# A mixture-of-experts layer stores its results by slot and gathers them by token

## What is computed

```python
logits = jnp.einsum('btc,ec->bte', x, router_w)
top_vals, top_idx = jax.lax.top_k(logits, TOP_K)          # TOP_K = 2
gates = jax.nn.sigmoid(top_vals)
w_full = jnp.zeros((N, E)).at[jnp.arange(N)[:, None], sel].add(gw)
gate, up = jnp.split(jnp.einsum('nc,ech->neh', xf, gate_up_w), 2, axis=-1)
out_all = jnp.einsum('neh,ehc->nec', silu(gate) * up, down_w)
moe = jnp.einsum('ne,nec->nc', w_full, out_all)
x = x + moe + shared                                      # then layer 1's attention reads layernorm(x)
```

## Time and profile before

| | |
|---|---|
| median of 3 runs | 944.12 us (941.67 to 946.22) |
| the profiled execution, its own time | 942.74 us |
| its span, first to last instruction | 940.3 us |
| mean granted TensorE clock | 0.964 |
| PE busy | 807.3 us (86%) |
| DVE busy | 607.4 us (65%) |
| ACT busy | 380.0 us (40%) |
| POOL busy | 238.6 us (25%) |
| POOL, gathers of line 1827 | 87 in both layers, 92.3 us |
| POOL, scatters of line 1834 | 48, 50.3 us |

### The profile page before, as it was taken

The page is one execution under the profiler, slowest core; times in us unless marked ns, Lnnn a source line. Parts: engine busy times, 40 slices in busy tenths (PEclk is TensorE's granted clock), DMA queues, the critical chain, the costliest instruction groups (busy, mean ns, idle before and its releaser), DMA issues.

```text
span 940.3 us, 23518 instructions
## 1 busy us (share of the span) xinstructions
PE 807.3 (86%) x8622; PEld 600.3 (64%) x8623; DVE 607.4 (65%) x1398; ACT 380.0 (40%) x750; POOL 238.6 (25%) x203
## 2 busy tenths in 40 slices
PE   5998998999977777779899999983659999999992
PEld 3655555655666666665545666663339899999992
DVE  3446777588645555555965888868965655555651
ACT  3325555533222212124314666666334444444440
POOL 0012000100146565651030000011034444444531
PEclk9999999999999999999997999996779999999997
DMA  8967302244442222228535411149232333333344
GB/s 265 104 82 114 125 3 71 88 148 154 135 136 84 73 80 77 78 73 222 88 45 73 90 47 48 47 161 381 91 123 56 71 72 70 68 68 68 72 66 112
DMA packets 72975, 94.68 MB, mean 101 GB/s; under 512 B 14321, under 2 KB 58225, under 8 KB 72881
## 3 DMA queue, kind: packets, MB, share of 16 engines
q1 hardware_dynamic: 57088, 62.17, 27.6%
q0 software_dynamic: 13872, 29.24, 12.4%
q10 hardware_dynamic: 1952, 2.39, 0.8%
HBM read 63.09 MB, written 19.92 MB: 88 GB/s over the span
## 4 chain that ended last, share of the span: by engine, by line
PE 60%; DVE 18%; issue 7%; another core or an unknown queue 5%; ACT 3%; DMA 2%; SPq 1%; DVEq 1%; POOLq 0%; ACTq 0%
PE bank L920 13%; PE bank L933 11%; PE bank L701 4%; PE bank L722 3%; PE bank L839 3%; PE bank L826 3%; PE bank L829 3%; PE bank L670 3%; PE bank L519 3%; PE bank L533 3%; PE bank L562 2%; DVE arena L1673 2%; DVE neg_max L1376 2%; DVE arena L1708 2%
## 5 line engine op out<-in xcount | busy, mean ns | idle before, releaser
L920 PE MATMUL bank<-arena 128*128 128x128 f16 x3024 | 303.8, 220 | 2.8 <-DVE arena L1678 2.0
L933 PE MATMUL bank<-arena 128*128 x1224 | 281.2, 273 | 5.1 <-DVE arena L1686 1.9
L920 PEld LDWEIGHTS bank<-arena 128*128 x3024 | 263.5, 98 | 20.4 <-issue 4.4
L1827 POOL DMA_INDIRECT arena<-xn_d,get_i x87 | 92.3, 1061 | 179.4 <-DVE arena L1673 79.1
L1241 ACT ACTIVATE arena<-bank,arena 128x128 f32<-128x128 f32 x312 | 85.9, 378 | 124.8 <-DMA arena<-in_exp_b 77.2
L1376 DVE TENSOR_REDUCE neg_max<-bank 128x2 f32<-128x512 f32 (+1 forms) x180 | 117.4, 684 | 28.0 <-PE bank L670 27.9
L933 PEld LDWEIGHTS bank<-arena 128*128 128x128 f16 x1224 | 119.4, 98 | 18.2 <-issue 16.6
L1111 ACT ACTIVATE arena<-bank 128x1024 f32<-128x1024 f32 x96 | 96.7, 1026 | 16.7 <-PE bank L688 16.1
L1837 POOL DMA_INDIRECT sum_d<-arena,put_i x39 | 64.0, 1642 | 111.2 <-DVE arena L1699 105.2
L1686 DVE TENSOR_TENSOR arena<-arena 128x512 f16<-128x512 f32 (+1 forms) x126 | 74.6, 592 | 4.3
L519 PE MATMUL bank<-consts 128*128 128x256 f32 (+2 forms) x144 | 53.5, 502 | 26.5 <-DVE slot L1577 18.0
(11 more groups left out here) (187 smaller groups left out, 1144.8 us busy)
## 6 DMA issues: line engine op xcount, KB each, us to landing
arena<-arena SPq DMA_DIRECT2D x96, 128.0 KB, 5.2
arena<-in_exp_up SPq DMA_DIRECT2D x16, 512.0 KB, 3.7
arena<-in_exp_dn SPq DMA_DIRECT2D x6, 1024.0 KB, 6.8
arena<-in_exp_up SPq DMA_DIRECT2D x5, 1024.0 KB, 5.9
arena<-in_exp_b SPq DMA_DIRECT2D x39, 128.0 KB
arena<-in_ctxT SPq DMA_DIRECT2D x8, 512.0 KB, 10.4
arena<-in_exp_dn SPq DMA_DIRECT2D x16, 256.0 KB, 4.0
xn_d<-arena POOLq DMA_DIRECT2D x8, 512.0 KB, 5.6
```

The source lines that it names most:

```text
L920: last = mm(upP[u][:, m // (UB // 2), m % (UB // 2) * P:(m % (UB // 2) + 1) * P], weights(e, 0, w, k * UPW[l] + m * P, P), rowsT[u][x][:, ...
L933: last = mm(yP[u], hidT[u][x][:, k], weights(e, 1, w, k * D, D), start=n == 0, stop=n == n_second - 1)
L1827: pool.indirect_dma_start(rows[i % 2], None, xn_d[l], bass.IndirectOffsetOnAxis(ap=get_i[:, i:i + 1], axis=0)).then_inc(s["rows_in"][i % 2 ...
```

## The change

Layer 0's results are no longer scattered. SP stores each tile as it is, 128 slots in a row of DRAM, with one plain DMA per tile, as soon as DVE has written it. POOL keeps only the gets in layer 0's loop; the puts of layer 1 are as before. At the start of layer 1 POOL, not SP, brings the results back: for each chunk, rank and token tile one indirect DMA that gathers 128 rows of `y_d` by `slot`, 32 in all. DVE's combine waits for all 8 of its chunk. The index arithmetic for empty slots falls away: they all fetch one of the first 128 tokens' rows, and nobody reads their results.

```diff
-        ranked_d = dram("ranked_d", (RANKED + 2 * N, D), F32)
+        y_d = dram("y_d", (NS[0] * P, D), F32)
...
-                if l:
-                    load_results(0, 2)
                 sp.wait_ge(once["far_set"], l + 1)
...
                     keys(1, 0)
-                    load_results(2, NC)
                     keys(1, 1)
...
-            def load_results(lo, hi):
+            def store_results():
                 s = B[0]
-                for u in range(RESULTS[0]):
-                    sp.wait_ge(s["y_stored"][u], (NS[0] + RESULTS[0] - 1 - u) // RESULTS[0] * 16)
-                for c in range(lo, hi):
-                    after(sp, s["gathered"][c % 2], c // 2 * 2 * 16)
-                    for i in range(2):
-                        sp.dma_start(y_got[c][:, i], by_token(ranked_d[RANKED + i * N:RANKED + (i + 1) * N], c)).then_inc(s["gathered"][c % 2], 16)
+                for i in range(NS[0]):
+                    sp.wait_ge(s["y_ready"], i + 1)
+                    sp.dma_start(y_d[i * P:(i + 1) * P], y_rows[i % 4]).then_inc(s["y_stored"][i % 4], 16)
...
                     load_context(1, 0, NC)
+                    store_results()
...
+                v.tensor_scalar(pad[0][:, 0:S], tile_of, 0.0, pcol[:], ALU.is_equal, ALU.mult)
                 if l:
-                    v.tensor_scalar(pad[0][:, 0:S], tile_of, 0.0, pcol[:], ALU.is_equal, ALU.mult)
                     v.tensor_scalar(pad[1][:, 0:S], tile_of, 0.0, float(N), ALU.is_equal, ALU.mult)
-                else:
-                    chain.then(v.tensor_scalar(pad[1][:, 0:S], tile_of, 0.0, None, ALU.is_equal))
-                    v.tensor_tensor(pad[0][:, 0:S], pad[1][:, 0:S], slot_no[:, 0:S], ALU.mult)
...
-                dve.wait_ge(s["gathered"][g % 2], (g // 2 + 1) * 2 * 16)
+                dve.wait_ge(s["gathered"][g % 2], (g // 2 + 1) * 2 * TC * 16)
...
+            def gather_results():
+
+                s = B[0]
+                for u in range(RESULTS[0]):
+                    pool.wait_ge(s["y_stored"][u], (NS[0] + RESULTS[0] - 1 - u) // RESULTS[0] * 16)
+                for c in range(NC):
+                    after(pool, s["gathered"][c % 2], c // 2 * 2 * TC * 16)
+                    for i in range(2):
+                        for t in range(TC):
+                            pool.indirect_dma_start(y_got[c][:, i, t], None, y_d, bass.IndirectOffsetOnAxis(
+                                ap=slot[:, i, c * TC + t:c * TC + t + 1], axis=0)).then_inc(s["gathered"][c % 2], 16)
...
+                if l:
+                    gather_results()
                 pool.wait_ge(once["bias_step"], l * 5 + 4)
...
-                for i in range(S + BEHIND):
+                for i in range(S + BEHIND if l else S):
                     if i < S:
                         get(i)
-                    if i >= BEHIND:
+                    if l and i >= BEHIND:
                         put(i - BEHIND)
```

More of the change, by code:

```diff
@@ L83, in dram @@
             return nc.dram_tensor(name, shape, dt, kind="Internal").ap()
-        RANKED = 48 * P
+        TOKENS = 48 * P
         xn_d = [dram(f"xn_d{l}", (N, D), F32) for l in range(2)]
-        ranked_d = dram("ranked_d", (RANKED + 2 * N, D), F32)
+        y_d = dram("y_d", (NS[0] * P, D), F32)
         sum_d = dram("sum_d", (N + P, D), F32)
@@ L198, in xattn_moe_program @@
         tile_col = sb("tile_col", [P, 2, 2 * T], I32)
-        slot_no = sb("slot_no", [P, 48])
         pad = [sb(f"pad{l}", [P, 48]) for l in range(2)]
@@ L1763, in _ @@
             v.tensor_copy(inv_val[:, :, 0], pcol[:].to_broadcast([P, 2 * T])).then_inc(once["iota_ready"], 1)
-            v.tensor_copy(inv_val[:, :, 1], iota_b[:, RANKED // P:RANKED // P + 2 * T]).then_inc(once["iota_ready"], 1)
-            v.tensor_scalar(slot_no[:], iota_b[:, 0:48], float(P), pcol[:], ALU.mult, ALU.add).then_inc(once["iota_ready"], 1)
-            dve.wait_ge(once["iota_ready"], 5)
+            v.tensor_copy(inv_val[:, :, 1], iota_b[:, TOKENS // P:TOKENS // P + 2 * T]).then_inc(once["iota_ready"], 1)
+            dve.wait_ge(once["iota_ready"], 4)
             for l in range(2):
@@ L1831, in put @@
                     pool.wait_ge(s["y_ready"], i + 1)
[L1832 to L1837, removed]
+                    after(pool, s["y_stored"][1 - i % 2], (i + 1) // 2 * 16)
+                    pool.indirect_dma_start(sum_d, bass.IndirectOffsetOnAxis(ap=put_i[:, i:i + 1], axis=0),
+                                            y_rows[i % 2], None, compute_op=ALU.add).then_inc(s["y_stored"][i % 2], 16)
                 BEHIND = 5
-                for i in range(S + BEHIND):
+                for i in range(S + BEHIND if l else S):
                     if i < S:
                         get(i)
-                    if i >= BEHIND:
+                    if l and i >= BEHIND:
                         put(i - BEHIND)
```

## The result

The changed kernel takes 934.34 us (median of 13 runs, 929.88 to 943.82) against 943.24 for the kernel before (13 runs, 937.84 to 951.97): ratio 0.9913, 95% interval 0.9884 to 0.9941. It is 0.9% faster and lies inside the range of 901 to 944, but 31 us were forecast and 9 came. The profiled execution took 932.53 us.

The account below looks back on a forecast made before the run. Layer 0's loop was taken to be bound by gathers queued behind POOL's scatters and late PE signals. Loop -38.6, gathers +6.9, clock +1: -30.7 from 942.74 gives 912.0, stated as 913 us; range 901 to 944.

Parts of the forecast that it names:

- Both causes named: Layer 0's expert loop: gathers queued behind scatters on POOL and late PE signals lengthen a step to 3.37 us.
- the first rival: Loop: PE's signals stay late, only the wait for rows goes; 925 to 943 us; chance 0.17.
- The third rival: Projection: DVE's operations hold up POOL's gathers; 917 us if mild, whole 38.6 gain eaten if severe, severe chance 0.04.
- chunk 0 is complete at 427.6 + 7 x 1.27 + 2.8: Projection: chunk 0's eight gathers, 1.27 us apart, the last landing 2.8 after issue, complete at 439.3.
- T + 45: Projection: fourth combine forecast to start about 45 us after T, the end of layer 0's last evacuation.
- the gathers' term: Projection: 32 gathers on POOL replacing SP's 8 loads cost 6.9 us; bounds 0 to 11.8.
- Chunk 3 ... 6.9 us late, and everything behind it in the projection hangs on that chunk: Projection: chunk 3's gathers complete at 469.8 against 462.95, delaying everything behind by 6.9 us.
- The 1 us for the clock: Projection: 1 us added for a lower granted clock after PE's new pauses; bounds 0 and 3.
- The second rival: Loop as long as before while gathers cost; 951 to 959 us, or down to 945; chance 0.12.

Follow-up runs that it names:

- session 3: Kernel before, unchanged, 943.61 us with late signals; beside it before again 943.82, changed 937.72, plain puts on POOL 938.02, gathers in bursts of 8 929.47.
- session 6: Kernel before 912.34 us with signals in time; beside it the changed kernel 917.65 and the changed kernel with gathers in bursts of 16 921.56.
- session 4: Kernel before 941.38 us with late signals; beside it changed 933.05, its gathers in bursts of 16 920.84, memset pauses between chunks 928.01.
- session 1: Kernel before 945.58 us, late signals; changed kernel with no gather 911.71, indirect stores on POOL 971.8, one gather in flight 979.26, stack copies held back 940.66.
- session 2: Kernel before 913.78 us, signals in time; changed kernel with bursts of 8 930.44, of 4 932.81, plain loads from POOL 910.51, plain puts 919.37.

## Why the prediction was right and wrong

**Right: the loop.** A step was forecast at 2.45 and is 2.51. Steps 4 to 44 save 34.5 us (forecast 36.8), step 44 1.06 (1.1). Step 4 begins 0.8 us later than in the trace of before, where 0.7 earlier was forecast; step 2 waits 0.94 us for its rows. (In the trace of the kernel before from session 3, step 4 begins at 279.15, as late as here, so this is not the change's doing.) Together, with the last steps, 35.1 of 38.6. Both causes named, rows queued behind scatters and late signals, went away with the scatters; the first rival, signals that stay late in the loop, is refuted. Where signals are in time the step goes only from 2.65 to about 2.5. So the late signals were the larger part of what the loop had to gain, and the queue the smaller.

**Right: the stores and the pace.** SP's store lands in 1.7 us, the first gather is issued 392.21 - 389.73 = 2.5 us after T (forecast 2.8), and the 32 gathers are (431.78 - 392.21) / 31 = 1.28 us apart (forecast 1.27). Each lasts 0.95 to 1.20 us. The third rival, gathers that crawl, is not seen here. By the rule of the Trainium skill, "SBUF — State Buffer", section "SBUF: two separate sides", GpSimd can't write descriptors while VectorE runs a two-port perf-mode operation. In this trace DVE's work beside the gathers costs at most 0.25 us a gather; which of its operations are of that kind no row says.

**A size: the landing.** The step "chunk 0 is complete at 427.6 + 7 x 1.27 + 2.8" took the landing of a single get. Eight on end are noticed 406.79 - 401.03 = 5.8 us after the last one's issue. Without late signals the fourth combine is at T + 47.8, not T + 45 (the prediction's 38.6 for before counts from the start of the last evacuation, its 45 from the end): the term is 9.5 us and not 6.9.

**Wrong: the gathers' term as a whole.** The step that failed is "Chunk 3 ... 6.9 us late, and everything behind it in the projection hangs on that chunk". It priced 32 indirect DMAs, 0.3 us apart, by POOL's own time. The prediction had named late signals as something that starts when indirect DMAs follow each other on POOL with 0.3 us between them, and then moved the same pattern, 32 in a row, to a place where PE, ACT and DVE pass each other work all the time. There it costs 26.2 - 9.5 = 16.7 us more, and the fourth combine hangs not on its chunk, which had landed, but on signals. The bounds of the term (0 to 11.8) did not hold the 26.2 measured. The 1 us for the clock is in part within these 26.2: the granted clock was 0.57 from 420 to 440, where PE idles, against 1.00 in the same stretch of session 6. The forecast missed the gain by 22 us: 3.5 in the loop, the rest here.

**Luck: the range.** Its upper end was moved from 925 to 944 to take in the first rival, signals that stay late in the loop. The 934 lies where that rival put it (925 to 943), but the loop's signals were in time; others, in the projection, were late.

**Wrong: the sign is not the kernel's alone.** The forecast took the late signals for a property of the kernel before. They depend on the condition of a session as well. The second rival, slower because of the gathers, holds where signals are in time, by its own rule: a step gains less than 0.2 us (2.65 to 2.51), which is less than the gathers cost. Why some sessions have late signals is open; the chip number is excluded, nothing else was tried. What delays a semaphore's change is open too: the runs show when it is late and what brings it on, not the mechanism. Nor does a count of DMAs on end explain all of it: in the loop POOL had only four on end (store, get, store, get) and then 1.76 us of idleness, and one signal in each such round was 1.7 to 2.0 us late, where eight gathers on end did nothing.

## What to carry to other kernels

Where the profile shows an effect with its trigger, ask of the change not only where the trigger goes away but where it is put: price the new place with the same effect. Where signals are late, breaking 32 gathers on POOL into bursts of 16 gained 12 us here; where they are in time it cost 4 (921.56 against 917.65). Plain DMAs, where rows lie in order, made no signal late in any run here. And take a fresh time of the old kernel beside each set of runs: here it moved by 30 us, three times what the change gained, and the sign of the change moved with it.

## What the hardware showed that was not expected

- ACT, free to copy PE's values, waited 14 to 23 us for the signal while POOL issued 32 indirect DMAs 1.26 us apart (18.24 in the changed kernel, 17.51 with the stack copies held back, 21.08 and 22.56 in its traces of sessions 4 and 3). With 16 on end the longest lag was 6.6, with 8 there was none. In the loop four on end, stores among them, were enough for 1.7 to 2.0. Plain stores of POOL between the gets caused none.
- What is late is the change of the semaphore (28.8 us behind PE's end in one case, session 4); the waiting engine starts right after it. An engine's signal to itself was 4.5 us late too.
- The issuing has to pause, not the landing to end: some 3 us of memsets between eights were enough. In layer 1's loop POOL issues two indirect DMAs 0.30 us apart and then waits 2.4 to 3.2 us; from the last evacuation of layer 0 to the end that kernel takes the same time, within 1 us, in both conditions.
- Whether it happens at all differs from session to session, on one and the same chip number: the kernel before took 907 to 914 in three sessions and 941 to 946 in three. Kernels without dense indirect DMAs seem not to care (911.71 in session 1 without gathers, 910.51 in session 2 with plain loads; no single one of them ran in both conditions).
- A gather of 128 rows of 1 KB is noticed 3.0 us after its issue when alone, 2.9 to 4.1 us at the end of four, and 5.8 us at the end of eight.
